# Query sine products moved from VectorE to ScalarE and GpSimd, with a fourth projection bank and queues that take over work a slot later

## The chip, the cores and the metric

The kernel runs on one core of a Trainium2 chip. A core has five engines that each work through their own instruction queue in order and meet only at semaphores: TensorE (PE, the matrix products), VectorE (DVE), ScalarE (ACT), GpSimd (POOL) and SyncE (SP, which here only issues DMAs). SBUF holds the operands, PSUM (eight banks of 128 x 512 fp32) the results of products. The metric is the device time of one execution in microseconds, lower is better.

## What is computed

A cross-attention block and a feed-forward layer, in fp32, on 32 sequences of 64 tokens of width 512:

```python
q = (layernorm(x) @ Wq)          # 32 heads of 128
k = (ctx @ Wk); v = (ctx @ Wv)   # 8 heads of 128, each shared by 4 query heads
q = q * cos + rotate_half(q) * sin          # rotate_half: [-q2, q1] of the two halves of a head
k = k * cos + rotate_half(k) * sin
p = softmax(where(mask == 0, -1e9, q @ k.T / sqrt(128)))
x = x + (p @ v) @ Wo
w = dequantize_mxfp4(quantize_mxfp4(ffn_kernel))   # blocks of 32
x = x + layernorm(x) @ w + bias
```

Here a head is laid with its 128 dimensions on the partitions and the tokens along the free axis, so `rotate_half` is an exchange of partitions 0 to 63 with 64 to 127, and its signs lie in the sine table.

## The kernel before

**Tiles and slots.** x and ctx are cut into 16 tiles of 128 tokens (two sequences). The work is done in two halves of 8 tiles, in each half for 8 key/value groups, in each group for 2 chunks of 4 tiles: 32 steps `s`, and 4 pairs in each, so 128 pairs. All engines run one loop over slots `n` from -4 to 140, written out by hand in each engine's block, and the order inside a slot is the order of the code. A slot is a pipeline stage of several pairs at once: TensorE projects query head `n` (`project_q`, 12 products of 128x512), computes the scores of pair m = n-5 (`scores`), turns the softmax of pair m-1 (`turn_p`), multiplies pair m-2 with the values (`values`) and projects the output of pair m-3 (`project_o`, 12 products). In every fourth slot (n % 4 = 1) it projects a key tile (`project_k`, 12 more), and in runs of 8 slots (3 to 10, 19 to 26, and so on) a value tile (`project_v`). fp32 precision is had by splitting each operand into a rounded high part and the rest (XH and XL, QH and QL, and so on): ScalarE makes the high part (`high`, L578), and GpSimd or VectorE subtracts it (`low`, L929).

**VectorE in a slot (before)**, L804 to L910: add the output product to `acc` (L815); multiply the query head in PSUM with cosine into `qT` (L724) and the two halves with sine into `t2` (L728, L729, `rotate`); mask (L843) and row maxima (L847) of pair m; the low part of the softmax (L856) and of the attention result (L860, `AL`); reciprocal and normalisation of pair m (L867, L869); then, where the slot has them, the key rotation, the low part of a value tile (L899, `VS`), up to three parts of the quantisation of the feed-forward weight (`quantise`, slots 10 to 55, on tile `F`), and the low parts of the normalised x (`x_low`) and of the feed-forward input (`f_low`).

**ScalarE in a slot (before)**: two early high parts of Wo if n is a multiple of 8 (`high(n, True)`); scaled scores of pair m from PSUM to `sm` (L619); softmax of pair m-1 into `PS` (L625, L628); high part of the attention result (L633, `AH`); four exponentials of pair m (L641); all other high parts (`high(n, False)`), the value tile (L657), and x or feed-forward tiles.

**GpSimd in a slot (before)**: the early low parts, the addition of `t2` to `qT` (L952), the other low parts, and in key slots the addition of `t2` to `kT`.

**Waits that matter.** `t2` is one buffer. Weight tiles come through a ring of two buffers (`raw`): the DMA of tile i waits for the low part of tile i-2. Every product that goes through `proj` takes the next of its banks in one fixed order (`bank_uses`), and `bank()` makes TensorE wait until the last reader of the earlier use is done (`freed`). Half way (slots 60 to 76) the second half's x and ctx tiles, masks and position rows are loaded and the first half's feed-forward layer is run and stored; SP issues `store(f)` only after `ffn_add(f)` (L718), and what stands behind it in its queue waits too.

## Time and profile before

| | |
|---|---|
| Median of 3 runs | 1244.49 us (1240.0 to 1246.65) |
| Profiled execution, own time | 1243.1 us |
| Its span, first to last instruction | 1240.9 us |
| TensorE busy | 1157.4 us (93%) |
| VectorE busy | 1032.9 us (83%) |
| ScalarE busy | 653.5 us (53%) |
| GpSimd busy | 503.4 us (41%) |

Busy shares are means over stages with different limits, so the stages matter: start (to 105 us, slots up to 9), quantisation (105.3 to 537.9 us, slots 10 to 58), half way (537.9 to 745.5 us, slots 59 to 76), the rest of the second half (745.5 to 1169.1 us, slots 77 to 126), and the end. A slot starts where the first product of its query head starts.

### The profile page before, as it was taken

How to read it: one execution, taken by the hardware profiler on the slowest of the kernel's cores; microseconds unless marked ns; L12 is line 12 of the kernel's file. 1: busy time of each engine (PE TensorE's matmuls, PEld its weight loads, DVE VectorE, ACT ScalarE, POOL GpSimd, SP SyncE). 2: the span in 40 equal slices, each digit the busy share in tenths (PEclk: the TensorE clock that was granted, in tenths of full speed). 3: DMA queues.
4: the chain of work that ended last, by engine and by line, in shares of the span. 5: the costliest groups of instructions: out<-in, count | busy, mean ns of one | idle time of the engine just before them, and what ended most of it. 6: DMA issues, size and time to landing. Idle time of an engine off the chain costs nothing.

```text
span 1240.9 us, 19680 instructions
## 1 busy us (share of the span) xinstructions
PE 1157.4 (93%) x6308; PEld 983.0 (79%) x6320; DVE 1032.9 (83%) x2003; ACT 653.5 (53%) x2169; POOL 503.4 (41%) x394
## 2 busy tenths in 40 slices
PE   3799989999999999997988999999999999999987
PEld 2578878887888878886777788888888888888864
DVE  5878999899989999878888887787777877777786
ACT  3255545555555555645453545555555655555561
POOL 5353443335342443445543434433353434342322
PEclk7999999999999999998998999999999999999999
DMA  5220111112111021112312223111021112110003
GB/s 171 77 77 23 52 43 43 48 31 60 39 41 42 27 68 40 51 45 89 108 54 74 77 86 93 45 35 35 26 60 36 43 27 60 30 48 18 26 26 102
DMA packets 41476, 67.41 MB, mean 54 GB/s; under 512 B 8992, under 2 KB 11168, under 8 KB 41376
## 3 DMA queue, kind: packets, MB, share of 16 engines
q1 hardware_dynamic: 40608, 64.05, 17.6%
q0 software_dynamic: 768, 2.10, 0.5%
q8 instruction: 53, 0.87, 0.3%
q14 instruction: 47, 0.39, 0.1%
HBM read 61.94 MB, written 4.19 MB: 53 GB/s over the span
## 4 chain that ended last, share of the span: by engine, by line
PE 66%; DVE 19%; ACT 4%; issue 4%; DMA 4%; POOL 2%; SPq 0%; ACTq 0%; DVEq 0%; POOLq 0%
PE proj L379 11%; PE proj L380 11%; PE proj L381 10%; PE pO L379 6%; PE pS L468 6%; PE pO L380 6%; PE pO L381 6%; DVE t L728 2%; DVE t L729 2%; PE pV L495 2%; DMA raw<-wo 2%; PE pV L496 2%; PE pT L478 2%; ACT sm L641 2%; PE pO L512 1%
## 5 line engine op out<-in xcount | busy, mean ns | idle before, releaser
L952 POOL TENSOR_TENSOR qT<-qT,t 128x512 f32<-128x512 f32 x128 | 187.3, 1463 | 393.3 <-DVE t L729 393.2
L619 ACT ACTIVATE sm<-pS 128x256 f32<-128x256 f32 x128 | 49.3, 385 | 313.7 <-PE pS L468 313.5
L641 ACT ACTIVATE sm<-sm,tiny 128x64 f32<-128x64 f32 x512 | 172.0, 337 | 77.0 <-DVE tiny L847 75.2
L379 PE MATMUL proj<-XH,QH 128*128 128x512 f32 x512 | 204.8, 400 | 6.1 <-DVE VS L899 4.1
L380 PE MATMUL proj<-XL,QH 128*128 128x512 f32 x512 | 202.6, 396 | 0.0
L381 PE MATMUL proj<-XH,QL 128*128 128x512 f32 x512 | 202.6, 396 | 0.0
L379 PE MATMUL pO<-OH,AH 128*128 128x512 f32 x448 | 181.1, 404 | 12.1 <-DVE acc L815 12.0
L380 PE MATMUL pO<-OL,AH 128*128 128x512 f32 x448 | 176.6, 394 | 0.0
L381 PE MATMUL pO<-OH,AL 128*128 128x512 f32 x448 | 175.9, 393 | 0.0
L468 PEld LDWEIGHTS pS<-kT,qT 128*128 128x128 f32 x1024 | 134.7, 192 | 13.2 <-issue 3.1
L724 DVE TENSOR_TENSOR qT<-proj,COS 128x512 f32<-128x512 f32 x128 | 88.0, 687 | 68.0 <-PE proj L381 40.2
L468 PE MATMUL pS<-kT,qT 128*128 128x64 f32 x1024 | 128.7, 269 | 2.7 <-ACT SIN L604 2.7
L929 POOL TENSOR_TENSOR QL<-raw,QH 128x512 fp32r<-128x512 f32 x64 | 85.0, 1328 | 96.3 <-ACT QH L578 96.3
L379 PEld LDWEIGHTS proj<-XH,QH 128*128 128x128 f32 x512 | 98.2, 192 | 27.2 <-DVE VS L899 4.7
L625 ACT CAST PS<-pT 64x256 fp32r<-64x256 f32 x256 | 93.9, 367 | 48.8 <-PE pV L496 45.3
L929 POOL TENSOR_TENSOR OL<-raw,OH 128x512 fp32r<-128x512 f32 x64 | 84.5, 1321 | 76.8 <-ACT OH L578 76.7
L728 DVE TENSOR_TENSOR t<-proj,SIN 64x512 f32<-64x512 f32 x160 | 111.0, 693 | 5.1 <-POOL kT L952 0.2
L381 PEld LDWEIGHTS proj<-XH,QL 128*128 128x128 f32 x512 | 98.0, 191 | 21.1
L380 PEld LDWEIGHTS proj<-XL,QH 128*128 128x128 f32 x512 | 98.2, 192 | 20.1
L729 DVE TENSOR_TENSOR t<-proj,SIN 64x512 f32<-64x512 f32 x160 | 109.4, 684 | 2.1
L856 DVE TENSOR_TENSOR PL<-pT,PS 64x256 fp32r<-64x256 f32 x256 | 106.7, 417 | 4.1
L379 PEld LDWEIGHTS pO<-OH,AH 128*128 128x128 f32 x448 | 85.4, 191 | 30.7 <-issue 14.6
(129 smaller groups left out, 2565.2 us busy)
## 6 DMA issues: line engine op xcount, KB each, us to landing
raw<-wq SPq DMA_DIRECT2D x64, 256.0 KB
raw<-wo SPq DMA_DIRECT2D x64, 256.0 KB
acc<-x SPq DMA_DIRECT2D x16, 256.0 KB, 3.0
raw<-wk SPq DMA_DIRECT2D x16, 256.0 KB
raw<-ctxT SPq DMA_DIRECT2D x16, 256.0 KB
raw<-wv SPq DMA_DIRECT2D x16, 256.0 KB
rawm<-fbias SPq DMA_DIRECT2D x16, 256.0 KB, 2.8
out<-acc SPq DMA_DIRECT2D x16, 256.0 KB, 2.0
```

The source lines that it names most:

```text
L379: pe.matmul(dst, lh, rh, start=k == 0, stop=False)
L380: pe.matmul(dst, lh, rl, start=False, stop=False)
L381: made = pe.matmul(dst, ll, rh, start=False, stop=k == last)
L468: made = pe.matmul(pS[:, 128 * hp + 64 * b:128 * hp + 64 * b + 64], qT[:, s % 2, 2 * p + b, 2 * hp:2 * hp + 2, :].rearrange("p h t -> p (h ...
L625: act.copy(PS[ROWS[i], i, :], pT[ROWS[i], 0:256]).then_inc(a_ph, 1)
L641: made = act.activation(v4[:, a], v4[:, a], ACT.Exp, bias=nmx[:, a:a + 1], accum_out=rsum[:, a:a + 1])
L724: dve.tensor_tensor(dst, src.rearrange("p (a t) -> p a t", t=64), COS[:, c].rearrange("p (a t) -> p a t", t=64), ALU.mult).then_inc(c_made, 1)
L728: dve.tensor_tensor(t2[0:64, :], src[64:128], SIN[64:128, c], ALU.mult)
L729: dve.tensor_tensor(t2[64:128, :], src[0:64], SIN[0:64, c], ALU.mult).then_inc(s_made, 1)
L856: dve.tensor_tensor(PL[ROWS[i], i, :], pT[ROWS[i], 0:256], PS[ROWS[i], i, :].bitcast(F32), ALU.subtract).then_inc(v_pl, 1)
L929: pool.tensor_tensor(lo, view(raw[:, i % RING, :]), hi.bitcast(F32), ALU.subtract).then_inc(g_lo, 1)
L952: pool.tensor_tensor(dst, dst, t2[:, :].rearrange("p (a t) -> p a t", t=64), ALU.add).then_inc(made, 1)
```

## The change

1. `PROJ` is 4 instead of 3. The bank comes from `pV`, whose two halves of 256 columns now share one bank.
2. The sine part of a query head leaves VectorE. ScalarE copies the two halves of the head from PSUM into `t2` exchanged (`exchange`, two 64x512 copies), and GpSimd multiplies `t2` with SIN in place and adds it to `qT` (`rotate_q`, two 128x512 operations). The bank of a query head is now free when `exchange` is done (`a_qx`), not after the second sine product. Keys stay on VectorE (subtracted by GpSimd, since the sine table has the other sign).
3. `exchange`, `rotate_q`, the value tile's high and low part, the tiles of x (one slot earlier in the table `X_AT`) and of the feed-forward input are done by their reader one slot after TensorE has made them, at the start of that slot.
4. Inside a slot, ScalarE does `high(n, False)` ahead of the scores and `AH` behind the exponentials; VectorE does quantisation ahead of the cosine product, `AL` behind the normalisation, and the key rotation last.

```diff
-PROJ = 3
+PROJ = 4
...
-X_AT = {-2: 4, -1: 5, 0: 6, 1: 7} | {HALF - 4 + t: 8 + t for t in range(8)}
+X_AT = {-2: 4, -1: 5, 0: 6, 1: 7} | {HALF - 5 + t: 8 + t for t in range(8)}
...
-        pV = pb("pV", [128, 2, 512])
+        pV = pb("pV", [128, 2, 256])
...
-            return {"x": (v_xl, i + 1), "q": (v_qs, i + 1), "k": (v_ks, i + 1), "v": (v_vl, i + 1),
+            return {"x": (v_xl, i + 1), "q": (a_qx, i + 1), "k": (v_ks, i + 1), "v": (v_vl, i + 1),
...
+            def exchange(i):
+
+                b = BANK["q", i]
+                act.wait_ge(v_qc, i + 1)
+                if i:
+                    act.wait_ge(g_qr, i)
+                else:
+                    act.wait_ge(e_ct, 4)
+                if i % 4 == 1:
+                    act.wait_ge(g_kr, i // 4 + 1)
+                act.copy(t2[0:64, :], proj[64:128, b, :])
+                act.copy(t2[64:128, :], proj[0:64, b, :]).then_inc(a_qx, 1)
+
             for n in range(FIRST, END):
                 m = n - 5
                 high(n, True)
+
+                if 0 <= n - 1 < PAIRS:
+                    exchange(n - 1)
+                if v_tile(n - 1):
+                    v_high(n - 1)
...
+                if n - 1 in X_AT:
+                    x_high(X_AT[n - 1])
+                if n - 1 in FFN_AT and not is_last(n - 1):
+                    f_high(FFN_AT[n - 1])
+                high(n, False)
+
                 if 0 <= m < PAIRS:
                     act.wait_ge(e_qk, m + 1)
...
-                if 0 <= m - 2 < PAIRS:
-                    act.wait_ge(e_pv, m - 1)
-                    if m - 2 >= 2:
-                        act.wait_ge(e_op, m - 3)
-                    act.copy(AH[:, m % 2].rearrange("p h (b t) -> p b h t", b=2),
-                             pV[:, :, 0:256].rearrange("p b (h t) -> p b h t", h=4)).then_inc(a_ah, 1)
                 if 0 <= m < PAIRS:
                     v4 = sm[:, m % 2, :].rearrange("p (a k) -> p a k", a=4)
...
                     made.then_inc(a_ex, 1)
+                if 0 <= m - 2 < PAIRS:
+                    act.wait_ge(e_pv, m - 1)
+                    if m - 2 >= 2:
+                        act.wait_ge(e_op, m - 3)
+                    act.copy(AH[:, m % 2].rearrange("p h (b t) -> p b h t", b=2),
+                             pV[:, :, :].rearrange("p b (h t) -> p b h t", h=4)).then_inc(a_ah, 1)
...
-                high(n, False)
...
-                if t2_freed:
-                    dve.wait_ge(*t2_freed)
-                dve.tensor_tensor(t2[0:64, :], src[64:128], SIN[64:128, c], ALU.mult)
-                dve.tensor_tensor(t2[64:128, :], src[0:64], SIN[0:64, c], ALU.mult).then_inc(s_made, 1)
+            def times_cos(b, dst, j0):
                 c = slice(512 * j0, 512 * j0 + 512)
...
-            def add_turned(dst, c_made, s_made, count, made):
-                pool.wait_ge(c_made, count)
-                pool.wait_ge(s_made, count)
-                pool.tensor_tensor(dst, dst, t2[:, :].rearrange("p (a t) -> p a t", t=64), ALU.add).then_inc(made, 1)
+            def rotate_q(i):
+
+                s, h = i // 4, i % 4
+                pool.wait_ge(a_qx, i + 1)
+                pool.tensor_tensor(t2[:, :], t2[:, :], SIN[:, 512 * (s % 2):512 * (s % 2) + 512],
+                                   ALU.mult).then_inc(g_qs, 1)
+                pool.wait_ge(g_qs, i + 1)
+                pool.wait_ge(v_qc, i + 1)
+                dst = qT[:, s % 2, :, h, :]
+                pool.tensor_tensor(dst, dst, t2[:, :].rearrange("p (a t) -> p a t", t=64), ALU.add).then_inc(g_qr, 1)
+
+            def rotate_k(s):
+
+                pool.wait_ge(v_kc, s + 1)
+                pool.wait_ge(v_ks, s + 1)
+                pool.tensor_tensor(kT[:, s % 2, :], kT[:, s % 2, :], t2[:, :], ALU.subtract).then_inc(g_kr, 1)
...
-                if 0 <= n < PAIRS:
-                    add_turned(qT[:, n // 4 % 2, :, n % 4, :], v_qc, v_qs, n + 1, g_qr)
+                if 0 <= n - 1 < PAIRS:
+                    rotate_q(n - 1)
+                low(n, False)
```

What this does to the order is best seen in a slot with a value tile in the quantisation stage. ScalarE before, from the scores of pair 30 (slot 35) to those of pair 31:

```order
L619 ACTIVATE sm<-pS 128x256
L625 CAST PS<-pT 64x256 x2
L628 CAST PS<-PS 64x256 x2
L633 CAST AH<-pV 128x2x4x64
L641 ACTIVATE sm,tiny<-sm,tiny 128x64 x4
L578 CAST OH<-raw 128x512
L657 CAST VS<-proj 64x256 x2
L619 ACTIVATE sm<-pS 128x256
```

ScalarE in the changed kernel, the same stretch (L637 and L638 are `exchange`, L619 is now the value tile, L583 a weight's high part):

```order
L664 ACTIVATE sm<-pS 128x256
L670 CAST PS<-pT 64x256 x2
L673 CAST PS<-PS 64x256 x2
L680 ACTIVATE sm,tiny<-sm,tiny 128x64 x4
L687 CAST AH<-pV 128x2x4x64
L637 COPY t<-proj 64x512
L638 COPY t<-proj 64x512
L619 CAST VS<-proj 64x256 x2
L583 CAST OH<-raw 128x512
L664 ACTIVATE sm<-pS 128x256
```

The exchange and the value tile now stand between the exponentials of one pair and the scores of the next. VectorE before, from one normalisation (slot 35) to the next row maxima (`F` is the quantisation):

```order
L869 TENSOR_TENSOR sm<-sm,tiny 128x256
L899 TENSOR_TENSOR VS<-proj,VS 64x256 x2
L772 SCALAR_TENSOR_TENSOR F<-F 128x256 x3
L815 TENSOR_TENSOR acc<-pO,acc 128x512
L724 TENSOR_TENSOR qT<-proj,COS 128x8x64
L728 TENSOR_TENSOR t<-proj,SIN 64x512
L729 TENSOR_TENSOR t<-proj,SIN 64x512
L843 COPY_PREDICATED sm<-mk,tiny 128x256
L847 TENSOR_REDUCE tiny<-sm 128x4
```

VectorE in the changed kernel, from the normalisation in slot 35 to the row maxima in slot 36:

```order
L906 TENSOR_TENSOR sm<-sm,tiny 128x256
L909 TENSOR_TENSOR AL<-pV,AH 128x2x4x64
L835 TENSOR_TENSOR acc<-pO,acc 128x512
L847 TENSOR_TENSOR VS<-proj,VS 64x256 x2
L792 SCALAR_TENSOR_TENSOR F<-F 128x256
L794 TENSOR_SCALAR tiny<-tiny 128x8
L796 TENSOR_TENSOR F<-F,tiny 128x256
L748 TENSOR_TENSOR qT<-proj,COS 128x8x64
L886 COPY_PREDICATED sm<-mk,tiny 128x256
L890 TENSOR_REDUCE tiny<-sm 128x4
```

The two sine products are gone and `AL` has come into the stretch; the value tile that is read is that of the slot before, and quantisation is that of the slot itself. ScalarE in the changed kernel half way, from the attention result of slot 71 to the scores of slot 72:

```order
L687 CAST AH<-pV 128x2x4x64
L583 CAST OH<-raw 128x512 x2
L637 COPY t<-proj 64x512
L638 COPY t<-proj 64x512
L619 CAST VS<-proj 64x256 x2
L599 CAST F<-proj 128x512
L664 ACTIVATE sm<-pS 128x256
```

The exchange of head 71 stands behind the two Wo tiles there; in the table of banks, heads 71, 72 and 73 each take the bank of the head just before them (four projections in each slot), so TensorE begins the head of slot 72 only when the exchange of head 71 is done.

## Rows read from the trace of the kernel before

**Rows 1.** The page, busy time (share of the span) and instructions of each engine.

```profile
PE 1157.4 (93%) x6308; PEld 983.0 (79%) x6320; DVE 1032.9 (83%) x2003; ACT 653.5 (53%) x2169; POOL 503.4 (41%) x394
```

**Rows 2.** Stretches: window, length, busy time of each engine (instructions), clock, DMA.

```profile
105.27:537.93 432.66, 418.63 (x2323) 361.56 (x2322) 394.85 (x786) 237.70 (x804) 168.86 (x122) 1.00 0.15 43
537.93:745.49 207.56, 183.45 (x965) 150.84 (x972) 174.22 (x324) 101.92 (x331) 97.42 (x83) 0.94 0.25 78
745.49:1169.11 423.62, 422.06 (x2346) 365.72 (x2344) 330.80 (x637) 238.47 (x804) 168.38 (x124) 1.00 0.15 43
```

**Rows 3.** Timeline of PE: first product of slots 84 to 86, 108 to 110.

```profile
802.48 0.39 PE L379 MATMUL proj<-XH,QH 128*128 128x512 f32 x1
...
810.93 0.39 PE L379 MATMUL proj<-XH,QH 128*128 128x512 f32 x1
...
822.12 0.39 PE L379 MATMUL proj<-XH,QH 128*128 128x512 f32 x1
...
1009.74 0.39 PE L379 MATMUL proj<-XH,QH 128*128 128x512 f32 x1
...
1016.74 0.39 PE L379 MATMUL proj<-XH,QH 128*128 128x512 f32 x1
...
1026.47 0.39 PE L379 MATMUL proj<-XH,QH 128*128 128x512 f32 x1
```

**Rows 4.** Waits of PE: line, line waited for, us in total, times, longest.

```profile
PE pO L379 <- DVE acc L815: 12.0, 10, 2.3
```

**Rows 5.** Groups by line and shape: count, busy us, mean ns, idle before.

```profile
L728 DVE TENSOR_TENSOR t<-proj,SIN 64x512 f32<-64x512 f32 x160 | 111.0, 693 | 5.1 <-POOL kT L952 0.2
...
L899 DVE TENSOR_TENSOR VS<-proj,VS 64x256 fp32r<-64x256 f32 x128 | 53.9, 421 | 19.9 <-ACT VS L657 18.5
...
L772 DVE SCALAR_TENSOR_TENSOR F<-F 128x256 f32<-128x256 f32 x32 | 22.2, 694 | 1.0
...
L633 ACT CAST AH<-pV 128x512 fp32r<-128x512 f32 x128 | 75.2, 587 | 5.9 <-PE pV L496 2.8
...
L952 POOL TENSOR_TENSOR qT<-qT,t 128x512 f32<-128x512 f32 x128 | 187.3, 1463 | 393.3 <-DVE t L729 393.2
```

**Rows 6.** Timeline of DVE: mask to normalisation of one pair (exponentials before L867).

```profile
438.06 0.46 DVE L843 COPY_PREDICATED sm<-mk,tiny 128x256 f32<-128x256 uint8 x1
438.55 0.42 DVE L847 TENSOR_REDUCE tiny<-sm 128x4 f32<-128x256 f32 x1
...
439.78 0.69 DVE L860 TENSOR_TENSOR AL<-pV,AH 128x512 fp32r<-128x512 f32 x1
440.47 0.18 DVE L867 RECIPROCAL tiny<-tiny 128x4 f32<-128x4 f32 x1
440.69 0.43 DVE L869 TENSOR_TENSOR sm<-sm,tiny 128x256 f32<-128x256 f32 x1
```

**Rows 7.** Timeline of POOL and DVE: quantisation steps with and without GpSimd at work.

```profile
432.28 1.42 POOL L929 TENSOR_TENSOR QL<-raw,QH 128x512 fp32r<-128x512 f32 x1 [1.39 <-ACT QH L578]
...
432.60 2.80 DVE L772 SCALAR_TENSOR_TENSOR F<-F 128x256 f32<-128x256 f32 x2
...
433.67 1.46 POOL L929 TENSOR_TENSOR KL<-raw,KH 128x512 fp32r<-128x512 f32 x1
...
485.11 1.34 DVE L772 SCALAR_TENSOR_TENSOR F<-F 128x256 f32<-128x256 f32 x3
```

**Rows 8.** Timeline of PE, SP's issues and ACT: slot 72, to slot 73's first product.

```profile
687.87 0.48 PE L379 MATMUL proj<-XH,QH 128*128 128x512 f32 x1
...
688.21 0.34 SPq L322 DMA_DIRECT2D out<-acc  x1
...
689.07 0.92 SPq L313 DMA_DIRECT2D raw<-wo  x2
...
694.95 0.62 ACT L578 CAST OH<-raw 128x512 fp32r<-128x512 f32 x1 [1.71 <-DMA raw<-wo]
...
701.65 0.50 PE L379 MATMUL proj<-XH,QH 128*128 128x512 f32 x1 [2.23 <-DVE VS L899]
```

More of the change, by code:

```diff
@@ L604, in rope, with v_high @@
                 act.copy(SIN[:, c], cs_turned(T)[:, 1, :]).then_inc(a_cs, 1)
+            def v_high(n):
+                s, t = v_tile(n)
+                v = v_count(s, t)
+                b = BANK["v", v - 1]
+                act.wait_ge(e_vp, v)
+                if s >= 2:
+                    act.wait_ge(e_pv, 4 * (s - 2) + t + 1)
+                for i in range(2):
+                    act.copy(VS[ROWS[i], i, 4 * (s % 2) + t, :], proj[ROWS[i], b, 0:256]).then_inc(a_vh, 1)
             for T in range(4):
@@ L819, in _ @@
                     statistics("f", FFN_AT[n])
+                if v_tile(n - 1):
+                    s, t = v_tile(n - 1)
+                    v = v_count(s, t)
+                    b = BANK["v", v - 1]
+                    dve.wait_ge(a_vh, 2 * v)
+                    for i in range(2):
+                        made = dve.tensor_tensor(VS[ROWS[1 - i], i, 4 * (s % 2) + t, :], proj[ROWS[i], b, 0:256],
+                                                 VS[ROWS[i], i, 4 * (s % 2) + t, :].bitcast(F32), ALU.subtract)
+                    made.then_inc(v_vl, 1)
+                if n - 1 in X_AT:
+                    x_low(X_AT[n - 1])
+                if n - 1 in FFN_AT and not is_last(n - 1):
+                    f_low(FFN_AT[n - 1])
+                for i in streamed(n, False):
+                    if lo_on_dve(i):
+                        _, kind, a, b = STREAM[i]
+                        hi, lo, _, view = weight(kind, a, b)
+                        dve.wait_ge(a_hi, i + 1)
+                        dve.tensor_tensor(lo, view(raw[:, i % RING, :]), hi.bitcast(F32),
+                                          ALU.subtract).then_inc(v_lo, 1)
+                for i, c in quant_parts(n):
+                    for step in PART[c] if c < 14 else ():
+                        quantise(i, step).then_inc(v_q, 1)
                 if 0 <= n < PAIRS:
@@ L885, in _ @@
                                       ALU.is_equal).then_inc(v_mk, 1)
+                if n - 1 in FFN_AT:
+                    ffn_add(FFN_AT[n - 1])
+                if is_last(n):
+                    f_low(FFN_AT[n])
                 if 0 <= n < PAIRS and n % 4 == 1:
@@ L890, in _ @@
                         dve.wait_ge(e_qk, 4 * (s - 2) + 4)
-                    rotate(BANK["k", s], kT[:, s % 2, :].rearrange("p (a t) -> p a t", t=64), s % 2, v_kc, v_ks,
-                           (g_qr, n + 1))
-                if v_tile(n):
-                    s, t = v_tile(n)
-                    v = v_count(s, t)
-                    b = BANK["v", v - 1]
-                    dve.wait_ge(a_vh, 2 * v)
-                    for i in range(2):
-                        made = dve.tensor_tensor(VS[ROWS[1 - i], i, 4 * (s % 2) + t, :], proj[ROWS[i], b, 0:256],
-                                                 VS[ROWS[i], i, 4 * (s % 2) + t, :].bitcast(F32), ALU.subtract)
-                    made.then_inc(v_vl, 1)
-                for i, c in quant_parts(n):
-                    for step in PART[c] if c < 14 else ():
-                        quantise(i, step).then_inc(v_q, 1)
-                if n - 1 in FFN_AT and n - 1 < PAIRS:
-                    ffn_add(FFN_AT[n - 1])
-                if n in X_AT:
-                    x_low(X_AT[n])
-                if n in FFN_AT and not is_last(n):
-                    f_low(FFN_AT[n])
+                    b, c = BANK["k", s], slice(512 * (s % 2), 512 * (s % 2) + 512)
+                    times_cos(b, kT[:, s % 2, :].rearrange("p (a t) -> p a t", t=64), s % 2).then_inc(v_kc, 1)
+                    dve.wait_ge(g_qr, n)
+                    dve.tensor_tensor(t2[0:64, :], proj[64:128, b, :], SIN[64:128, c], ALU.mult)
+                    dve.tensor_tensor(t2[64:128, :], proj[0:64, b, :], SIN[0:64, c], ALU.mult).then_inc(v_ks, 1)
         @block.gpsimd
```

80 lines of the change are left out of this document (27 added, 53 removed).

## The prediction

> **What bounds the kernel now.** I read the page's busy shares first, then the stretches, then how far apart the first products of the slots lie. TensorE is busy for 93% of the span [rows 1], and every other engine has room on average, so a gain can only come out of places where TensorE is not fed. The stretches say where those are [rows 2]. The first products of neighbouring slots give TensorE's own floor for a slot [rows 3]: 802.48 to 810.93 is 8.45 us with a value tile, 810.93 to 822.12 is 11.19 with value and key, 1009.74 to 1016.74 is 7.00 for a plain slot, 1016.74 to 1026.47 is 9.73 with a key. Counted over the slots of each stretch: slots 10 to 58 have 19 value, 6 value and key, 18 plain and 6 key slots, floor 412.1 us, and take 432.7, so 20.6 over. Slots 77 to 126 (18, 6, 19 and 7) have a floor of 420.3 and take 423.6, 3.3 over. Slots 59 to 76 (6, 2, 8 and 2) have 148.6 and take 207.6, 59.0 over, a good third of which is real work that other slots lack (64 feed-forward products, 16 tiles to transpose) and some of it a clock of 0.94 in place of 1.00. The change adds no work to TensorE and takes none away. So some 24 us outside the half-way stretch can be won, and anything that makes another engine's round longer than the floor is lost.
>
> **VectorE's round in the quantisation stretch.** VectorE is busy 394.9 of 432.7 us there, 91%, against 330.8 of 423.6, 78%, later [rows 2], and TensorE's largest named wait there is for `acc` [rows 4]. VectorE is the second bound, and only in this stretch. Its round, from one pair's row maxima to the next, in a plain slot before: 1.50 from the end of the maxima (438.97) to the reciprocal (440.47), in which `AL` fits, 0.65 for reciprocal and normalisation [rows 6], quantisation, `acc` 0.69, cosine 0.69, two sine products 1.38 (all three at the price of that shape [rows 5]), mask 0.46, maxima 0.42. Quantisation without waiting I estimate at 1.3 us a slot (20 steps per tile of 5.67 slots; a wide step is 1.34 / 3 = 0.45 [rows 7], the narrow ones less). Sum 7.1. A run of 8 slots with two keys (2.07 each) is 60.9 bare, the floor is 6 x 7.00 + 2 x 9.73 = 61.5, and measured it is 61.5 + 20.6 / 3 = 68.4, if all of the 20.6 lies in the three plain runs. The rest, 0.9 us a slot, is waiting.
>
> **Where that waiting comes from** decides the forecast. Two quantisation steps took 2.80 us while GpSimd ran two low parts, three took 1.34 with GpSimd idle [rows 7]: the first ended 0.3 us after GpSimd's first operation, the second 0.3 us after its second. A step with all operands in SBUF that begins under a GpSimd operation waits for its end. A sine product reads PSUM, and its mean is 693 ns with GpSimd at work or not. By this row the change gives up work on VectorE that never waited and makes GpSimd hold what VectorE's SBUF steps need for two more long operations' time. The Trainium skill (SBUF — State Buffer, "SBUF: two separate sides") calls the pair of ports that VectorE and GpSimd share an exclusive lock held for the whole instruction, which speaks against this change too. Had they shared bandwidth instead, the waiting below would shrink and the first rival would hold; the trace agrees with the lock.
>
> **Part 1, sine products off VectorE.** It removes 2 x 0.69 = 1.38 us a slot from VectorE [rows 5]. `AL`, however, moves behind the normalisation, out of the 1.50 us in which it was hidden: +0.69. Plain round: 1.50 + 0.65 + 0.69 + 0.69 + 1.3 + 0.69 + 0.46 + 0.42 = 6.4, a run 8 x 6.4 + 4.1 = 55.3, so 0.78 us of waiting a slot would be free. GpSimd gets a 128x512 multiplication beside its addition; no row has it, the low parts give 1.42 to 1.46 [rows 7], the addition 1.46 [rows 5], so `rotate_q` is 2.9 us. ScalarE gets two 64x512 copies from PSUM; the nearest row is 0.59 for 128x512 [rows 5], so 1.17 (between 0.6, if half the partitions cost half, and 1.3). It starts after `AH`, 1.45 + 0.59 after the maxima, ends at 3.2, and GpSimd is busy from 3.2 to 6.1. Quantisation now starts at 1.50 + 0.65 + 0.69 + 0.69 = 3.5: it lies under `rotate_q` in every slot, and a low part often follows. Two steps that wait cost the rest of the multiplication and the whole addition, up to 2.6 us; slots with no or narrow steps pay little. I take 1.5 us a slot, with ends at 0.7 (as before the change) and 2.0. Then a run is 55.3 + 12 = 67.3, 5.8 over, against 6.9 before: -3 us for three runs (ends -21 and +9).
>
> **Part 2, the value tile a slot later.** This adds a round that was not there. VectorE reads the value tile's high part before quantisation and cosine, ScalarE makes it behind `exchange`, that stands behind `AH`, and that behind the exponentials, which wait for VectorE's maxima. One turn: exponentials 1.45, `AH` 0.59, exchange 1.17, the value tile's two copies 0.75 (from `AH` by columns; 0.6 to 1.2), its low part 2 x 0.42 = 0.84 [rows 5], quantisation 1.3, cosine 0.69, mask 0.46, maxima 0.42: 7.7 us against a floor of 8.45. In a key slot the exchange of its head waits for the key's addition: 0.65 + 0.69 + 3 x 0.69 + 1.46 in place of `AH`'s 0.59, +4.3, where TensorE's key costs only 2.74. A run: 8 x 7.7 + 2 x 4.3 = 70.2 against 73.1, so only 0.36 us a slot is free. Quantisation starts 4.8 after the maxima, under GpSimd's addition and the low parts. With 1.3 us (0.7 to 2.0) the 21 value slots that quantise lose 21 x 0.94 = +20 (+7 to +34). Before, the value runs sat on their floor. Both parts together: +17, ends -14 and +43.
>
> **Part 3, half way.** In slots 70 to 75 a slot uses four banks, so heads 71 to 73 take the bank of the head before and TensorE waits for its exchange. For head 71 this stands behind two Wo tiles, whose DMAs SP issues only after the store that waits for `ffn_add`: store at 688.21, tiles from 689.07, second tile cast at 695.57 [rows 8], 7.4 us after the store. With the store some 9.5 us into slot 71 (it needs TensorE's feed-forward product and `AL`) the exchange ends at 18 and slot 72 starts at 10.6, so TensorE stands for about 7 us. Slot 72 took 13.8 us before [rows 8] against 10.6 of work, so 3 of that is paid already: +4. In slots 69 and 73 the transposed feed-forward input takes the bank of that slot's own head, whose exchange waits for the key's rotation: +1 and +3. Sum +8 (0 to +12). In the x phase the normalisation comes 1.4 us earlier and the fourth bank helps, but third and fourth weight tiles of slots 62 and 64 now hold ScalarE up ahead of the scores: -4 (-12 to +6).
>
> **The rest.** Slots 77 to 126 have no quantisation: the value round is 6.4 and 10.7 against 8.45 and 11.19, and TensorE hides it; Wo's third and fourth tile are loaded earlier, -2 (-3 to +6, the latter if the key slots' late exchange pushes the scores). Start 0 (-5 to +4), end +1, since four scores wait for the last `rotate_q`. pV in one bank costs nothing, since `values` already waits for `AL`.
>
> **Sum**: -3 + 20 + 8 - 4 - 2 + 0 + 1 = +20 on 1243.1, the profiled execution's own time (1.4 us under the median of the three): 1263 us.
>
> **Rivals.** (a) Relief wins: the waiting stays near 0.7 us because most steps slip into the gaps between GpSimd's operations. Then quantisation gives -14, x -8, half way +4, the rest -3: 1222 us. For it: VectorE at 91% is what the change empties. Against it: where quantisation starts. (b) The two cancel: waiting of about 0.9 gives -5 in quantisation, half way and x +4: about 1243 us, no change. (c) The waiting is whole, 2.0: 1243 + 43 + 5 = 1291 us. It decides from a waiting of 0.36 us in a value slot on.
>
> **How the numbers follow.** Chances: forecast 0.50 (1250 to 1280), (a) 0.22, (b) 0.18, (c) 0.10. A measurement of this kernel tells about 0.5% from no change, so between 1238 and 1250 is the same. Slower: 0.50 + 0.10 = 0.60, same 0.18, faster 0.22. The range leaves out (c) and the lower half of (a): 1223 to 1284.
>
> **What would show it.** Right: value slots of 19 to 55 at 9 us and more with VectorE's value tile waiting for ScalarE, L772's successor at over 0.9 us in the mean, a stop of TensorE of 5 us or more at the start of slot 72, slots 77 to 126 still at 8.45 and 7.00. Wrong: value slots at 8.45 in the quantisation stretch, or steps whose mean stays near 0.69; or late slots off their floor, which I have not priced.

## The result and the profile after

The changed kernel takes 1312.0 us (median of 4 runs, 1311.4 to 1316.4) against 1243.1 us (1240.0 to 1246.7, 4 runs) of the kernel before on the same chip: 1.056 times the time, 95% interval 1.052 to 1.060. The profiled execution has a span of 1310.0 us, 69.1 us longer than before. The direction was right; the forecast, 1263 us, and the top of the range, 1284 us, were both too low.

The page after, busy time of each engine and the chain that ended last, answers to [rows 1]:

```profile
PE 1183.2 (90%) x6308; PEld 1001.3 (76%) x6320; DVE 925.9 (71%) x1747; ACT 807.7 (62%) x2425; POOL 648.9 (50%) x522
...
PE 49%; DVE 20%; ACT 11%; issue 9%; POOL 6%; DMA 4%; SPq 1%; ACTq 0%; DVEq 0%; POOLq 0%
```

VectorE was relieved of 107 us and the kernel got slower. TensorE does the same 6308 instructions in 25.8 us more, and its share of the chain is down from 66% to 49%. The stretches answer to [rows 2] (window, length, then PE, PEld, DVE, ACT and POOL busy, clock, DMA share, GB/s): slots 10 to 58, 59 to 76, 77 to 126.

```profile
102.69:583.74 481.05, 441.16 (x2324) 375.48 (x2323) 384.32 (x689) 295.28 (x903) 224.08 (x171) 0.96 0.13 38
583.74:808.86 225.12, 187.00 (x965) 154.07 (x972) 145.92 (x285) 124.01 (x367) 118.62 (x102) 0.91 0.22 73
808.86:1234.62 425.76, 423.37 (x2345) 367.82 (x2344) 280.75 (x538) 300.65 (x908) 225.00 (x173) 1.00 0.14 42
```

Against the floors of [rows 3] (412.1, 148.6 and 420.3 us) the excess went as follows; the last two columns are the forecast and its ends.

| Slots | before | after | change | forecast | ends |
|---|---|---|---|---|---|
| 0 to 9, with the start | 105.3 to begin of slot 10 | 102.7 | -2.6 | 0 | -5, +4 |
| 10 to 58 | 20.6 over | 69.0 over | +48.4 | +17 | -14, +43 |
| 59 to 76 | 59.0 over | 76.6 over | +17.6 | +4 | -12, +18 |
| 77 to 126 | 3.3 over | 5.4 over | +2.1 | -2 | -3, +6 |
| after slot 127 begins | 71.8 | 75.4 | +3.6 | +1 | |

Waits of TensorE (line, line waited for, us in total, times, longest) name the new releaser, L638, the second copy of `exchange`, in place of `acc` [rows 4]:

```profile
PE proj L382 <- ACT t L638: 25.6, 9, 5.8
PE proj L396 <- DVE qT L721: 20.8, 3, 9.4
PE pS L418 <- issue: 20.4, 6, 7.6
PE pT L483 <- DVE sm L906: 14.3, 18, 1.8
...
PE pO L382 <- DVE acc L835: 6.8, 6, 1.5
```

Groups by line (busy us, mean ns, idle before and its releaser), from two views of after, the page and the groups by shape; they answer to [rows 5]:

```profile
L974 POOL TENSOR_TENSOR t<-t,SIN 128x512 f32<-128x512 f32 x128 | 164.8, 1288 | 278.5 <-ACT t L638 277.0
L979 POOL TENSOR_TENSOR qT<-qT,t 128x512 f32<-128x512 f32 x128 | 168.4, 1316 | 10.0
L637 ACT COPY t<-proj 64x512 f32<-64x512 f32 x128 | 74.6, 583 | 154.9 <-POOL kT L985 145.8
```

```profile
L792 DVE SCALAR_TENSOR_TENSOR F<-F 128x256 f32<-128x256 f32 x32 | 34.0, 1064 | 0.9
L886 DVE COPY_PREDICATED sm<-mk,tiny 128x256 f32<-128x256 uint8 x128 | 104.3, 815 | 55.3 <-ACT sm L664 54.6
L904 DVE RECIPROCAL tiny<-tiny 128x4 f32<-128x4 f32 x128 | 22.8, 178 | 104.0 <-ACT sm L680 103.5
```

The quantiser's comparison, the same 32 instructions as L772 [rows 5], went from 694 to 1064 ns in the mean. It does no more work; it waits inside its own duration. And VectorE now stands idle for 103.5 us ahead of the reciprocal, where it was 33.5 us before. Timeline of VectorE and GpSimd in slot 35 (start, us, engine, line; `x3` is three steps in a row), where [rows 7] had 1.34 us for three steps alone:

```profile
350.11 1.29 POOL L974 TENSOR_TENSOR t<-t,SIN 128x512 f32<-128x512 f32 x1 [1.60 <-ACT t L638]
350.13 4.42 DVE L792 SCALAR_TENSOR_TENSOR F<-F 128x256 f32<-128x256 f32 x3
351.48 1.36 POOL L979 TENSOR_TENSOR qT<-qT,t 128x512 f32<-128x512 f32 x1
352.80 1.47 POOL L950 TENSOR_TENSOR OL<-raw,OH 128x512 fp32r<-128x512 f32 x1
354.47 0.68 DVE L748 TENSOR_TENSOR qT<-proj,COS 128x512 f32<-128x512 f32 x1
```

Three steps took 4.42 us because three GpSimd operations stood back to back: the multiplication, the addition and a low part. The cosine, and behind it mask and maxima, began 3 us later than they had to.

All 160 quantisation steps together are busy 76.7 us before and 128.8 us after (sums over the quantiser's rows). At their undisturbed durations (0.17 us narrow, 0.29 and 0.42 us wide) they would be 50 us. So the waiting grew from 26 to 78 us, by about what slots 10 to 58 lost.

### The profile page after: what moved, and what is told of

It is laid out like the page before. It is cut to its first block, busy times and chain, and to the rows that moved or that the text cites. A ratio compares the mean times of both kernels' runs of the same rounds, so it can differ in the third digit from the quotient of the medians.

```text
span 1310.0 us, 19935 instructions
## 1 busy us (share of the span) xinstructions
PE 1183.2 (90%) x6308; PEld 1001.3 (76%) x6320; DVE 925.9 (71%) x1747; ACT 807.7 (62%) x2425; POOL 648.9 (50%) x522
## 4 chain that ended last, share of the span: by engine, by line
PE 49%; DVE 20%; ACT 11%; issue 9%; POOL 6%; DMA 4%; SPq 1%; ACTq 0%; DVEq 0%; POOLq 0%
PE proj L382 8%; PE proj L383 8%; PE proj L384 8%; ACT sm L680 5%; PE pO L382 4%; PE pS L473 4%; PE pO L383 4%; PE pO L384 4%; DVE sm L886 3%; POOL kT L985 2%; DVE AL L909 2%; DVE qT L748 2%; PE pV L500 1%; DMA raw<-ctxT 1%; PE pO L517 1%
## 5 line engine op out<-in xcount | busy, mean ns | idle before, releaser
L974 POOL TENSOR_TENSOR t<-t,SIN 128x512 f32<-128x512 f32 x128 | 164.8, 1288 | 278.5 <-ACT t L638 277.0
L382 PE MATMUL pO<-OH,AH 128*128 128x512 f32 x448 | 183.8, 410 | 6.8 <-DVE acc L835 6.8
L383 PE MATMUL pO<-OL,AH 128*128 128x512 f32 x448 | 179.7, 401 | 0.0
L384 PE MATMUL pO<-OH,AL 128*128 128x512 f32 x448 | 178.6, 399 | 0.0
L979 POOL TENSOR_TENSOR qT<-qT,t 128x512 f32<-128x512 f32 x128 | 168.4, 1316 | 10.0
L637 ACT COPY t<-proj 64x512 f32<-64x512 f32 x128 | 74.6, 583 | 154.9 <-POOL kT L985 145.8
L886 DVE COPY_PREDICATED sm<-mk,tiny 128x256 f32<-128x256 uint8 x128 | 104.3, 815 | 55.3 <-ACT sm L664 54.6
L382 PEld LDWEIGHTS proj<-XH,QH 128*128 128x128 f32 x512 | 98.6, 193 | 34.9 <-ACT t L638 15.0
L985 POOL TENSOR_TENSOR kT<-kT,t 128x512 f32<-128x512 f32 x32 | 41.0, 1282 | 167.9 <-DVE t L931 167.9
L847 DVE TENSOR_TENSOR VS<-proj,VS 64x256 fp32r<-64x256 f32 x128 | 54.0, 422 | 85.5 <-ACT VS L619 84.4
```

The costliest lines, as they stand in the source:

```text
L382: pe.matmul(dst, lh, rh, start=k == 0, stop=False)
L383: pe.matmul(dst, lh, rl, start=False, stop=False)
L384: made = pe.matmul(dst, ll, rh, start=False, stop=k == last)
L886: dve.copy_predicated(v.rearrange("p (h k) -> p h k", h=2), mk[:, j:j + 1, :].broadcast_to([128, 2, 128]), neg.unsqueeze(2).broadcast_to([ ...
L974: pool.tensor_tensor(t2[:, :], t2[:, :], SIN[:, 512 * (s % 2):512 * (s % 2) + 512], ALU.mult).then_inc(g_qs, 1)
L979: pool.tensor_tensor(dst, dst, t2[:, :].rearrange("p (a t) -> p a t", t=64), ALU.add).then_inc(g_qr, 1)
```

## The experiments

All excesses below are over the same floors. "Wide steps" is VectorE's busy time on the quantiser's tile `F` in slots 10 to 58, 104 instructions in each kernel: 59.0 us before, 96.0 us after; at their undisturbed durations they would be 41 us.

### Without quantisation

```diff
-                    return dve.tensor_scalar(B, A, 5.0, 2.0, ALU.is_gt, ALU.mult)
...
+                    return dve.memset(B, 0.0)
```

The other steps of a tile become memsets of a single element, so a tile keeps twenty short instructions (19 of one element and the one shown), not the three that the text below speaks of. In the changed kernel:

> The changed kernel with the twenty quantisation steps of each weight tile on VectorE replaced by three memsets (so the quantisation arithmetic is left out and the feed-forward result is not the reference's). The feed-forward products, all loads and every wait stay. In the changed kernel slots 10 to 58 take 481.1 us against a floor of 412.1. Theory 1 (the loss there is VectorE's round: its quantisation steps, each waiting under GpSimd's now 2.6 us long rotation, in series with value tile, cosine, mask and maxima): that stretch falls to 415 to 425 us and the whole to about 1250 us. Theory 2 (TensorE waits for banks, since a head's bank is now freed by ScalarE's copies a slot later): the banks don't change, the stretch stays above 455, the whole above 1285 us. Theory 3 (ScalarE's longer list is the round by itself): as theory 2, above 1285 us.

Measured: 1256.4 us, slots 10 to 58 8.5 us over the floor. Slots 59 to 76 stay at 79.1. The kernel before with the same edit:

> The kernel before with the same replacement of the quantisation steps by memsets (quantisation arithmetic left out). Slots 10 to 58 take 432.7 us there, 20.6 over the floor. Theory 1: at most those 20.6 us go, the whole comes to 1222 to 1230 us; the difference between the two kernels without quantisation is then 20 to 30 us (half way, end) in place of 69. Theories 2 and 3: the difference stays above 55 us.

Measured: 1227.8 us, 5.4 over. The two kernels differ by 28.6 us then. What is lost in slots 10 to 58 is lost only with VectorE's steps in the round; all the rest of the change, banks and ScalarE's longer list among it, costs 3 us there by itself. The other 20 us of half way are separate.

### Without GpSimd's multiplication

```diff
-                pool.tensor_tensor(t2[:, :], t2[:, :], SIN[:, 512 * (s % 2):512 * (s % 2) + 512],
-                                   ALU.mult).then_inc(g_qs, 1)
```

> The changed kernel without GpSimd's multiplication with SIN (the sine part of the queries is added without its factor, so the output is not the reference's). rotate_q is then one operation of 1.3 us in place of two. Theory 1 with the waiting under GpSimd as its main part: about half of the 48 us lost in slots 10 to 58 comes back, 20 to 30 us, the whole 1280 to 1292 us. Rival (the length of the serial round through exchange and value tile, without GpSimd's part): no more than 8 us comes back, from the key slots, 1302 to 1312 us.

Measured: 1280.5 us (1.031, 1.029 to 1.034), slots 10 to 58 38.1 over, wide steps 79.8. One of the two long operations is worth 31 us of the 69. The 160 steps' busy time fell by 26 us (128.8 to 102.9), and that of the mask in these slots by 5 us (0.66 to 0.56 us each).

### One more GpSimd operation in the kernel before

The counter-test: the same load on GpSimd, in the old order.

```diff
+                if made is g_qr:
+                    pool.tensor_tensor(t2[:, :], t2[:, :], t2[:, :], ALU.mult).then_inc(g_m, 1)
+                    pool.wait_ge(g_m, count)
                 pool.tensor_tensor(dst, dst, t2[:, :].rearrange("p (a t) -> p a t", t=64), ALU.add).then_inc(made, 1)
```

> The kernel before with one more GpSimd operation in each slot: t2 multiplied with itself in place ahead of the queries' addition (the output is not the reference's), so that GpSimd's rotation is 2.6 us long as in the changed kernel, while VectorE still makes the sine products and the value tiles are loaded in their old slot. Slots 10 to 58 have 20.7 us over the floor before. Theory 1 (quantisation steps wait under GpSimd's second long operation): 15 to 35 us more there, the whole 1256 to 1278 us, with the mean of the quantisation steps (0.54 us for the mask of the quantiser's forms now) going up. Rival (the extra multiplication only hurt because ScalarE's exchange, value tile and exponentials stand in one row with it): under 6 us more, 1240 to 1248 us.

Measured: 1244.2 us, 1.003 times the kernel before (1.001 to 1.004); slots 10 to 58 22.3 over. The rival's numbers came, and theory 1, as I had put it, falls: 128 more operations of 1.2 us cost 3.4 us. The groups by line of this run show them, and the window over slots 10 to 58 for tile `F` alone (length, VectorE busy, count, clock, DMA share, GB/s) shows that the steps don't notice:

```profile
L954 POOL TENSOR_TENSOR t<-t 128x512 f32<-128x512 f32 x128 | 155.2, 1212 | 372.7 <-DVE t L730 372.6
```

```profile
107.49:541.88 434.39, 58.97 (x104) 1.00 0.15 43
```

Before, the same window has 58.99. In the old order this operation follows VectorE's sine products, and VectorE then does mask, maxima, `PL` and `AL`. The mask mostly gets in first (524 ns in the mean, 542 before); the other three read PSUM or have one operand, and stay at 0.42 and 0.69 us under it. So GpSimd's load alone does not cost this. What differs in the changed kernel is the time at which it runs: the rotation starts off ScalarE's exchange, which ends when VectorE comes to its steps. The Trainium skill (SBUF — State Buffer, "SBUF: two separate sides") has VectorE take the shared ports only with two SBUF inputs or in a two-port mode; the trace agrees, with at most 0.694 us for `AL` here, though 123 of the 128 run under a GpSimd operation, and 1.4 us for a 0.42 us step in the changed kernel.

### Sine products back on VectorE

```diff
-                if 0 <= n - 1 < PAIRS:
-                    exchange(n - 1)
...
+                    dve.tensor_tensor(t2[0:64, :], proj[64:128, b, :], SIN[64:128, c], ALU.mult)
+                    dve.tensor_tensor(t2[64:128, :], proj[0:64, b, :], SIN[0:64, c], ALU.mult).then_inc(a_qx, 1)
...
-                if 0 <= n - 1 < PAIRS:
-                    rotate_q(n - 1)
+                if 0 <= n < PAIRS:
+                    rotate_q(n)
```

> The changed kernel with one part undone: the query sine products stand on VectorE again, directly behind the cosine, ScalarE has no exchange, and GpSimd only adds, in the head's own slot. Value tiles a slot later, the new order of all queues and four projection banks stay. Theory 1: the loss is that of the sine products' move, so the time comes back to 1240 to 1255 us. Rival (value tiles a slot later and the new order make the round longer by themselves): it stays at 1280 us or more, since VectorE has 1.38 us a slot more to do again.

Measured: 1281.4 us (1.032, 1.028 to 1.035); slots 10 to 58 32.9 over, slots 59 to 76 72.0. The rival's number (1280 us or more) came, theory 1's did not, and neither describes it: the steps now wait hardly at all (wide steps 45.5 us, the comparison 465 ns), so 36 us come back, and yet 33 us stay.

```profile
L790 DVE SCALAR_TENSOR_TENSOR F<-F 128x256 f32<-128x256 f32 x32 | 14.9, 465 | 0.9
...
L911 DVE RECIPROCAL tiny<-tiny 128x4 f32<-128x4 f32 x128 | 22.8, 178 | 85.3 <-ACT sm L678 84.6
```

The second row says where to look: VectorE idles 84.6 us ahead of the reciprocal, where `AL` no longer lies. That gave the second theory, which the next run tests.

### `AH` and `AL` back under the exponentials

```diff
+                if 0 <= m - 2 < PAIRS:
+                    dve.wait_ge(a_ah, m - 1)
+                    dve.tensor_tensor(AL[:, m % 2].rearrange("p h (b t) -> p b h t", b=2),
...
                 if 0 <= m < PAIRS:
                     v4 = sm[:, m % 2, :].rearrange("p (a k) -> p a k", a=4)
                     dve.wait_ge(a_ex, m + 1)
```

> The changed kernel with one part undone: ScalarE's AH stands ahead of the exponentials again, and VectorE's AL ahead of the reciprocal, under VectorE's wait for the exponentials (37.6 us of idle time at L904 in slots 10 to 58). Theory (the sine products left VectorE, but AL left the cover it had, so VectorE gained only half of what was taken off): 0.6 to 0.7 us a slot come back in slots 10 to 58, 20 to 33 of their 69 us over the floor, the whole 1278 to 1292 us. Rival (VectorE's idle time is not what counts, only when GpSimd's rotation runs): under 8 us come back, and since AH now waits ahead of the exponentials it can be a loss.

Measured: 1274.6 us (1.028, 1.027 to 1.030), slots 10 to 58 34.9 over, a little more than expected. The reciprocal's idle time falls from 104.0 to 43.9 us, while the steps wait nearly as before (comparison 919 ns against 1064):

```profile
L910 DVE RECIPROCAL tiny<-tiny 128x4 f32<-128x4 f32 x128 | 22.7, 177 | 43.9 <-ACT sm L686 43.2
```

### Both undone together

> Both causes undone together: the changed kernel with the query sine products on VectorE (slots 10 to 58 fell from 69.1 to 33.0 us over the floor by that) and AH and AL under the exponentials again (69.1 to 34.9), and the high parts of third and fourth tiles behind AH in slots 59 to 76. If these two are separate causes in slots 10 to 58 (steps that wait under GpSimd, and AL without cover), the stretch comes to 5 to 16 us over the floor, what is left being key slots, and the whole to 1240 to 1252 us. If they are one and the same slack counted twice, it stays at 25 to 33 and the whole above 1258 us. If the value tiles a slot later are a third cause, the value slots 19 to 26, 35 to 42 and 51 to 58 keep more than 6 us over the floor.

Measured: 1239.9 us (0.998, 0.997 to 0.999), slots 10 to 58 11.0 over, the three value runs 1.1 us together. Two causes, then, and no third in these slots: 36.1 and 34.1 us each by itself, 58.0 together. The sum is more than the whole; a slot that is back on its floor can't gain again. Value tiles taken over a slot later cost nothing there by themselves. The stretch is even better than in the kernel before (20.6). Most of that is not the order of VectorE's queue: this kernel has ScalarE's early high parts, and they alone bring the kernel before to 14.8 (a run below). Slots 0 to 9 are 8 us longer than before in this kernel and in the one with only the sine products back; why is open.

### Quantisation in the gap

The steps go behind the softmax's low part, into the idle time that `AL` left:

```diff
-                for i, c in quant_parts(n):
-                    for step in PART[c] if c < 14 else ():
-                        quantise(i, step).then_inc(v_q, 1)
...
                                           ALU.subtract).then_inc(v_pl, 1)
+                for i, c in quant_parts(n):
+                    for step in PART[c] if c < 14 else ():
+                        quantise(i, step).then_inc(v_q, 1)
                 if 0 <= m < PAIRS:
                     v4 = sm[:, m % 2, :].rearrange("p (a k) -> p a k", a=4)
                     dve.wait_ge(a_ex, m + 1)
```

> The changed kernel with the quantisation steps moved on VectorE from ahead of the cosine to behind the softmax's low part, ahead of the reciprocal, where VectorE waits for ScalarE's exponentials. Theory 1: the steps leave the serial stretch between value tile and maxima, and part of them falls into VectorE's wait, so slots 10 to 58 give back 25 to 45 of their 69 us over the floor: 1268 to 1288 us. Rival (they then begin under GpSimd's low parts or the rotation all the same and push the normalisation, on which GpSimd doesn't hang but TensorE's transposes do): within 8 us of the changed kernel.

Measured: 1268.0 us (1.020, 1.017 to 1.024), slots 10 to 58 20.7 over: 48 us back, all that was lost there. One move treats both causes: the gap is filled, and there GpSimd is not at its rotation (wide steps 47.9 us). The mask, which now comes earlier, waits instead (0.90 us in the mean in these slots, 0.66 in the changed kernel), and half way is 80.5 over.

### Half way: who holds the scores up

Timeline of SP's issues, ScalarE and TensorE in slot 62 of after:

```profile
623.27 0.33 SPq L316 DMA_DIRECT2D raw<-ctxT  x1
...
625.99 0.62 ACT L583 CAST CH<-raw 128x512 fp32r<-128x512 f32 x1 [6.21 <-DMA raw<-ctxT]
626.51 0.38 ACT L664 ACTIVATE sm<-pS 128x256 f32<-128x256 f32 x1
...
626.99 0.66 PE L418 MATMUL pS<-ident,F 128*128 128x128 f32 x2 [7.64 <-issue]
```

The ring frees a buffer for the context tile only at 623.27, ScalarE waits 6.21 us for it with the scores behind, and TensorE, whose next product writes the scores' bank, stands 7.64 us. Putting the high parts back behind `AH` in every slot:

```diff
-                high(n, False)
-
                 if 0 <= m < PAIRS:
                     act.wait_ge(e_qk, m + 1)
...
                              pV[:, :, :].rearrange("p b (h t) -> p b h t", h=4)).then_inc(a_ah, 1)
+                high(n, False)
```

> The changed kernel with ScalarE's high parts of the third and fourth weight tiles of a slot put back behind the exponentials and AH, as in the kernel before. Half way (slots 59 to 76) the changed kernel has 76.6 us over the floor, before 59.0; in slots 62 and 64 it loses 13.3 and 9.6 us where ScalarE waited 6.2 us for the DMA of a context tile with the scores behind it. Theory (these waits ahead of the scores are the loss of slots 60 to 68): 9 to 16 us come back there, slots 62 and 64 each under 5 us. Rival (the DMA itself is late, and whoever waits, the slot ends no earlier): under 4 us come back, the wait turns up at TensorE's context transposes. Outside half way no more than 5 us either way.

Measured: 1319.6 us, slower than the changed kernel. Slots 60 to 65 give back 12.0 us (32.8 to 20.7), and slots 62 and 64 come to 9.0 and 7.3, not under 5 as expected. But slots 66 and 69 lose 8.5 us, and the start and slots 77 to 126 another 8.5, which was to be 5 at most. As a remedy it fails; as a cause it was still to be shown. The kernel before with the fourth bank alone (`PROJ = 4`, pV in one bank), and that with the high parts ahead of the scores:

> The kernel before with the fourth projection bank alone, pV in one bank. Theory: the banks are worth 0 to 8 us half way, where a slot fills four, and nothing else (1235 to 1243 us); pV in one bank costs nothing. Rival: values(m) and AL now stand in one bank and TensorE waits for AL in each slot, 0.1 to 0.4 us a slot, 1245 to 1265 us.

Measured: 1238.0 us (0.998, 0.997 to 0.999), slots 59 to 76 54.8 over in place of 59.0, slot 72 at 2.4 in place of 5.3; elsewhere nothing.

```diff
                 high(n, True)
+                if n >= 10:
+                    high(n, False)
                 if 0 <= m < PAIRS:
```

> The kernel before with four banks (alone: slots 59 to 76 54.8 us over the floor) and the high parts of third and fourth weight tiles ahead of the scores in every slot from 10 on, half way too. Sine products, value tiles, x tiles and transposed feed-forward tiles stay where they were. Theory (ScalarE's waits for a weight tile's DMA ahead of the scores cost half way by themselves): slots 60 to 65 lose 6 to 12 us against the run with four banks, so slots 59 to 76 come to 61 to 68 us over the floor. Rival (they only cost together with tiles taken over a slot later): within 3 us of 54.8.

Measured: 1245.4 us, slots 59 to 76 65.6 over, 10.8 more than with the banks alone: +12.3 in slots 60 to 65, 3.2 given back in 66 to 68. Slots 60 to 68 are then 39.0 over, as in the changed kernel (39.0; before 30.0). The same stop, without any of the rest of the change:

```profile
568.45 0.33 SPq L313 DMA_DIRECT2D raw<-ctxT  x1
...
571.21 0.62 ACT L580 CAST CH<-raw 128x512 fp32r<-128x512 f32 x1 [6.62 <-DMA raw<-ctxT]
571.74 0.38 ACT L623 ACTIVATE sm<-pS 128x256 f32<-128x256 f32 x1
...
572.21 0.66 PE L415 MATMUL pS<-ident,F 128*128 128x128 f32 x2 [8.31 <-issue]
```

The changed kernel with the sine products on VectorE and the high parts late in slots 59 to 76:

> The changed kernel with the query sine products on VectorE again (1281.4 us; slots 59 to 76 72.0 us over the floor) and with the high parts of third and fourth tiles behind AH in slots 59 to 76. What is then left of the change half way is the takeover a slot later, of value, x and feed-forward tiles. Theory of two causes: 6 to 10 us come back in slots 60 to 65 and the stretch stays at 62 to 66, 7 to 11 above the 54.8 of the kernel before with four banks; this rest is the later takeover. If the order of the high parts is the whole of it: 54 to 58.

Measured: 1265.9 us, slots 59 to 76 59.9 over: 12.1 back, and 5.1 above the run with four banks, less than the 7 to 11 I expected. So half way splits, from the kernel before through these runs to the changed one (59.0, 54.8, 65.6, 72.0, 76.6), into -4.2 for the bank, +10.8 for the early high parts, +6.4 for the rest without the sine products, by name the tiles taken over a slot later, and +4.6 for the sine products' move. The last two are differences between runs, not seen apart; by slots, the sine products' move is +6.7 in slots 69 to 76, where slot 71 goes from 2.2 to 8.0, and -2.1 in slots 60 to 68.

### Exchange ahead of the early Wo tiles

```diff
-                high(n, True)
-
                 if 0 <= n - 1 < PAIRS:
                     exchange(n - 1)
+                high(n, True)
```

It is aimed at slot 72 (SP's issues, ScalarE, TensorE in after; [rows 8] before):

```profile
742.47 0.34 SPq L325 DMA_DIRECT2D out<-acc  x1
...
743.33 0.93 SPq L316 DMA_DIRECT2D raw<-wo  x2
...
746.76 1.29 ACT L583 CAST OH<-raw 128x512 fp32r<-128x512 f32 x2 [5.70 <-DMA raw<-wo]
748.07 0.58 ACT L637 COPY t<-proj 64x512 f32<-64x512 f32 x1
...
749.29 0.80 PE L382 MATMUL proj<-XH,QH 128*128 128x512 f32 x1 [5.52 <-ACT t L638]
```

> The changed kernel with ScalarE's exchange of the last head ahead of the high parts of a slot's first two weight tiles. In slot 72 these are two Wo tiles that wait 5.7 us for their DMA, and TensorE then waits 5.5 us for the head's bank. Theory: slots 69 to 73 give back 5 to 9 us, the whole 1300 to 1308 us, and slots 77 to 126 stay at their floor. Rival (in all other slots a first tile's high part is now later, and TensorE's next head with it): the gain half way is lost again in slots 10 to 58.

Measured: 1318.9 us. Slot 71, at whose end the stop lies, falls from 8.0 to 2.2 us over, slots 69 to 73 together only from 29.6 to 26.2, less than the 5 to 9 us expected, and slots 10 to 58 lose 7.2: the rival.

### Three edits at once

Quantisation in the gap, the exchange ahead of the early Wo tiles from slot 59 on, and the high parts back behind `AH` in slots 59 to 76.

> The changed kernel with three edits at once: the quantisation steps behind the softmax's low part (alone 1268.0 us), and from slot 59 on the exchange ahead of the slot's first high parts, and in slots 59 to 76 the high parts of third and fourth tiles behind AH. If half way is a matter of ScalarE's order, slots 59 to 76 fall from 80.5 us over the floor to 60 to 68 and the whole to 1250 to 1258 us. If the loss there comes from the x tiles, the transposed feed-forward tiles and the value tiles being taken over a slot later, it stays above 72.

Measured: 1254.9 us (1.013, 1.011 to 1.014), slots 10 to 58 20.8 and slots 59 to 76 66.8 over. Half way is partly ScalarE's order; slot 69 alone is 14.3 over, where the changed kernel has 8.4.

### What of the change is worth keeping

The early high parts in slots 10 to 58 of the kernel before:

> The kernel before with one thing of the change alone: ScalarE's high parts of a slot's third and fourth weight tiles stand ahead of the scores, in slots 10 to 58 only. GpSimd's low parts then run under the maxima and the softmax's low part instead of under the quantisation steps. In the kernel before the steps wait 27.7 us in these slots. Theory (it is where GpSimd works when the steps are due, and with sine products on VectorE the earlier low parts get out of their way, as in the run with the sine products back, where the steps' waits are 6 us): 8 to 15 us come back, the whole 1228 to 1236 us, the mean of the quantiser's comparison row from 0.69 to under 0.5 us. Rival (the scores stand behind a weight tile's DMA instead): no gain or a loss of up to 10 us.

Measured: 1236.1 us (0.9958, 0.9945 to 0.997), slots 10 to 58 14.8 over (20.6), wide steps 53.4 us, the comparison 583 ns. The direction holds, but the mean was to fall under 500 ns and the gain to be 8 us or more; it is 5.8. With the fourth bank:

> The kernel before with four banks and the early high parts in slots 10 to 58 alone. The two gains were 2.6 us half way and 4.5 us in slots 10 to 58, in different stretches, so they should add up: 1232 to 1235 us, 0.5% under the kernel before. If the one takes the other's room, 1236 to 1238.

Measured: 1233.2 us, ratio 0.9935 (0.992 to 0.995): faster than both kernels. The stretches of this kernel, as above:

```profile
105.34:532.53 427.19, 418.78 (x2324) 363.15 (x2322) 386.54 (x786) 240.34 (x804) 164.69 (x122) 1.00 0.15 44
532.53:737.20 204.67, 183.75 (x973) 150.87 (x972) 174.57 (x324) 101.72 (x331) 97.16 (x83) 0.94 0.26 79
```

And from slot 0 on:

> As the kernel before with four banks and early high parts in slots 10 to 58, with the early high parts from slot 0 on. Slot 8 had 2.9 us over the floor before and none in the changed kernel. Theory: it is a weight tile late by ScalarE's order, and 2 to 4 us come back in slots 0 to 9 (78.5 before). Rival: in the first slots the third and fourth tiles' DMAs are the late ones, and the scores wait for them: 0 to 5 us lost.

Measured: 1233.5 us (0.992 to 0.995). Slot 8 falls from 2.9 to 0.5 us over, but slot 10 begins no earlier (105.9 us), so the 2 to 4 us did not come: within its interval the same.

## Why the prediction was wrong in size

**Right.** The reading of the bounds [rows 1 to 4], the lock between VectorE's SBUF steps and GpSimd [rows 7], and the bare rounds. Put the waiting that was measured into them and they give the time: a plain run of eight slots 55.3 + 8 x 2.1 = 72.1 against 73.4, 74.0 and 71.7 us; the first two value runs 70.2 + 8 x 1.8 = 84.6 against 86.9 and 86.4 (the third, which quantises in five of its slots only, took 80.2). The signs by which I wanted to be judged came: most of the value slots without a key from 19 to 55 take 9.0 us or more (13 of 16), VectorE's value tile waits for ScalarE in 25 slots (34.4 us), the comparison is over 0.9 us, TensorE stops 5.52 us at slot 72, late slots stand at 8.45 and 7.00.

**The step that failed** is the waiting per slot, 1.5 us in a plain and 1.3 in a value slot. The steps waited 1.8 in plain and 1.7 in value slots, and the mask, which also works in SBUF and which I had left at 0.46, another 0.3 and 0.1: 2.1 and 1.8 us a slot. That is rival (c), waiting 2.0, to which I gave 0.10; its +43 for this stretch is near the +48.4. The forecast had +20 for value slots and -3 for plain ones; measured +33 and +16. I had reasoned that slots with narrow steps pay little. They pay the same: a 0.17 us step (L770) took up to 1.22 us under a 1.3 us operation. GpSimd's rotation itself was sized too long, at 2.9 us; it took 2.6 (1.29 and 1.32), so the miss is not there.

**Steps with the right sign and a wrong account.** Relief by 1.38 us and `AL` out of its cover at +0.69 were both in the sum. But I weighed the first as the gain of the change and the second as its small print, while the run without it is 37 us faster. Read as a price of its own, 0.69 us in each of 49 slots is 34 us, and 34.1 is what came back.

**Half way.** The bank's exchange behind the early Wo tiles: +8 forecast, +8 measured in slots 69 to 76. That the two agree is in part luck. By the runs above, the sine products' move gives +6.7 there, the fourth bank -4.2, the early high parts +1.7 and the rest +3.8; I had priced only waits for the exchange. The x phase, slots 60 to 68: -4 forecast, +9.1 measured. I had named the held-up scores of slots 62 and 64 and set a gain against them; the early high parts cost 9.1 us there by themselves, and all the rest of the change adds up to nothing in these slots. The end of the range for it, +6, was too low as well.

**Not in the sum: TensorE's clock.** Before, none of the 1320 products of 128x512 in slots 10 to 58 took over 0.51 us; after, 62 took over 0.5, in nine places, each behind a wait of TensorE of 0.95 to 5.76 us. Windows of after in slot 62 (columns as above): the end of the stop, the 4.8 us behind it, and a stretch right after.

```profile
622.00:629.40 7.40, 0.66 (x2) 0.29 (x2) 2.45 (x4) 2.89 (x10) 4.73 (x5) 0.50 0.15 44
629.40:634.20 4.80, 4.71 (x13) 3.89 (x14) 2.12 (x6) 3.58 (x13) 0.00 (x0) 0.50 0.52 179
634.60:642.00 7.40, 7.40 (x42) 6.34 (x41) 5.59 (x10) 3.37 (x12) 4.85 (x5) 1.00 0.02 4
```

The granted clock is 0.50 in the first two, its lower level of 1.2 GHz, and 1.00 in the third; a product then comes every 0.43 us in place of 0.23. For 62 products that is 12 us of TensorE's time. It isn't apart from the rest: it comes and goes with the waits (10 such products with quantisation in the gap, 11 with both causes undone). Where VectorE's round is the bound it may fall into time that TensorE would wait anyway. How much of it counts is open.

## What to carry to other kernels

Before an operation is moved from VectorE to GpSimd, look up what VectorE does at the time at which GpSimd will run it. In this case, under operations that mostly read PSUM, 1.2 us a slot more cost 3 us in all, under SBUF steps 31. And an operation that lay in another engine's wait is free only there: moved out of it, it is paid in full, which here ate half of the relief. A copy that waits for a DMA should be put ahead of the critical operation in its queue only in stretches where its DMA has long landed. Of the two parts of this change that gain, the fourth bank does so as it is (1238.0 us), the early high parts only so placed: with both, 1233.2 us where they keep to slots 10 to 58, 1245.4 where they go on half way.

## What the runs showed of the hardware that I had not expected

A narrow VectorE step pays as much as a wide one. On 128x8 elements L770 takes 0.17 us alone and up to 1.22 under a GpSimd operation, and the wait stands within the instruction's own duration, so no wait row shows it; a mean against the shortest of its kind does.

GpSimd is held up in its turn. Its addition took 1463 ns in the mean before [rows 5]. In 120 of the 128 slots VectorE's mask had begun just ahead of it, and there it took 1.44 to 1.49 us; in the run without the multiplication it also starts from idle, but not under the mask, and takes 1286 ns. VectorE and GpSimd in slot 40 before:

```profile
376.93 0.45 DVE L843 COPY_PREDICATED sm<-mk,tiny 128x256 f32<-128x256 uint8 x1
377.04 1.46 POOL L952 TENSOR_TENSOR qT<-qT,t 128x512 f32<-128x512 f32 x1 [1.40 <-DVE t L729]
```

And TensorE came back from its stops of 5.76 us (slot 22) and 7.64 us (slot 62) at the lower clock, with 0.63 us for each of ten and of eight 128x512 products in a row.
